# Rotating queries and keys with neighbouring pairs, a swap in two transfers, and another order of normalising

## The reference, cut to what matters

```python
h = layernorm(x) * ln_scale + ln_bias
c_q, c_kv = h @ w_down_q.T, h @ w_down_kv.T            # latents, 128 wide
q, k, v = c_q @ w_up_q.T, c_kv @ w_up_k.T, c_kv @ w_up_v.T   # 16 heads of 64
e, o = q[..., 0::2], q[..., 1::2]                      # the same for k
q = stack([e * cos - o * sin, e * sin + o * cos], -1)  # rotary, all 64 columns
out = softmax(q @ k.T / 8) @ v @ w_out.T + x
```

## Time and profile before

| | us |
|---|---|
| median of 3 runs | 1969.89 (1966.94 to 1970.7) |
| the profiled execution's own time | 1970.43 |
| its span, first to last instruction | 1968.7 |
| loop of `stage_a` in it | about 223 to 1151 |
| busy PE, DVE, ACT, POOL in 216 to 1136 | 887, 603, 391, 771 |

### The profile page before, as it was taken

One profiled execution on the slowest core, in us unless ns is written; L12 is line 12 of the kernel. 1 busy time (PEld: TensorE's weight loads), 2 busy tenths in 40 slices (PEclk: granted clock), 3 DMA queues, 4 the chain that ended last, 5 costly groups with the idle time before them and its releaser, 6 DMA issues. The chain is left out here.

```text
span 1968.7 us, 35663 instructions
## 1 busy us (share of the span) xinstructions
PE 1796.7 (91%) x12884; PEld 1290.1 (66%) x12884; DVE 1222.3 (62%) x1863; ACT 941.0 (48%) x1613; POOL 1255.2 (64%) x816
## 2 busy tenths in 40 slices
PE   5999699998999999999999978988975999998998
PEld 4888344554555555555555546666654999998998
DVE  5676566666666666756667537767752666655343
ACT  5876344434344443444434324333322567775554
POOL 3463599877788888888889734554651654435433
PEclk9999899999999999999999999999986999999999
DMA  4333322233231323332232221222336233323232
GB/s 146 107 124 125 94 50 70 59 88 97 76 86 33 97 65 76 87 76 63 56 88 67 50 92 57 81 78 82 86 99 250 44 81 93 87 44 82 40 47 40
DMA packets 92930, 160.63 MB, mean 82 GB/s; under 512 B 16188, under 2 KB 66652, under 8 KB 89428
## 3 DMA queue, kind: packets, MB, share of 16 engines
q1 hardware_dynamic: 73920, 121.69, 22.7%
q0 software_dynamic: 14592, 18.40, 5.6%
q10 hardware_dynamic: 4288, 18.81, 2.6%
HBM read 80.06 MB, written 44.71 MB: 63 GB/s over the span
## 5 line engine op out<-in xcount | busy, mean ns | idle before, releaser
L1215 ACT ACTIVATE a_pr<-a_pT 128x1024 f32<-128x1024 f32 x256 | 262.6, 1026 | 421.7 <-PE a_pT L954 421.7
L1073 DVE TENSOR_REDUCE a_row_max<-a_pG 128x2 f32<-128x1024 f32 x256 | 310.4, 1215 | 110.7 <-PE a_pG L924 110.5
L1250 POOL TENSOR_TENSOR a_total<-a_total,a_pr 128x1024 f32<-128x1024 f32 x128 | 316.2, 2470 | 16.1 <-ACT a_pr L1215 8.6
L2288 DVE TENSOR_TENSOR c_h_lo<-c_h,c_h_hi 128x256 fp32r<-128x256 f32 x288 | 151.7, 532 | 182.7 <-ACT c_h_hi L2243 178.0
L967 PE MATMUL a_pA<-a_pr,a_v 128*64 128x512 f32 x1024 | 248.1, 605 | 0.0
L2243 ACT ACTIVATE c_h<-c_pU,c_b_c 128x256 f32<-128x256 f32 x288 | 141.3, 491 | 172.0 <-PE c_pU L105 171.0
L1231 POOL TENSOR_TENSOR a_by_cos<-a_by_cos,a_swapped 128x1024 f32<-128x1024 f32 x64 | 151.6, 2369 | 105.6 <-DMA a_swapped<-a_by_sin 105.6
L1250 POOL TENSOR_TENSOR a_total<-a_pr 128x1024 f32<-128x1024 f32 x64 | 166.3, 2598 | 40.2 <-ACT a_pr L1215 40.2
L1238 POOL TENSOR_TENSOR a_qk_lo<-a_by_cos,a_qk_hi 128x1024 fp32r<-128x1024 f32 x64 | 154.7, 2418 | 2.3 <-ACT a_qk_hi L1184 2.3
L2341 POOL DMA_INDIRECT out_x<-c_y,c_ids x72 | 119.1, 1654 | 41.0 <-DVE c_y L2304 28.5
L924 PE MATMUL a_pG<-a_qk_hi 64*128 64x512 f32 x512 | 117.2, 456 | 29.9 <-ACT a_qk_hi L1184 18.5
(11 more groups left out here) (297 smaller groups left out, 4861.0 us busy)
## 6 DMA issues: line engine op xcount, KB each, us to landing
a_swapped<-a_by_sin SPq DMA_DIRECT2D x256, 128.0 KB, 2.3
a_inv_by_head<-mid_inverses SPq DMA_DIRECT2D x30, 512.0 KB, 6.5
c_raw<-in_weights ACTq DMA_DIRECT2D x5, 2048.0 KB, 8.3
c_x_t<-mid_rows SPq DMA_DIRECT2D x36, 272.0 KB, 2.8
mid_latents<-f_c_parts SPq DMA_DIRECT2D x8, 1024.0 KB, 4.7
first_latents<-mid_latents SPq DMA_DIRECT2D x8, 1024.0 KB, 5.1
f_x_t<-in_x SPq DMA_DIRECT2D x8, 512.0 KB, 3.8
mid_part<-f_out SPq DMA_DIRECT2D x16, 256.0 KB, 2.4
```

What stands on the lines that cost most here:

```text
L1073: nc.vector.reduce_max(row_max[:, u % 2, :, t], pair[:], AX.X).then_inc(read, 1)
L1215: nc.scalar.activation(pr[:, n % RP, :, :], pT[:], ACT.Exp, scale=SCALE).then_inc(exp_done, 1)
L1250: nc.gpsimd.tensor_tensor(total[:, u % RT, :, :], before, pr[:, n % RP, :, :], ALU.add).then_inc(summed, 1)
L2288: nc.vector.tensor_tensor(h_lo[:, m % RH, :], h[:, m % RH, :], h_hi[:, m % RH, :], ALU.subtract).then_inc(h_lo_done[m % RH], 1)
```

## The change: what it does

1. On the host, `w_up_q` and `w_up_k` are no longer reordered: the even and odd column of a pair lie on neighbouring partitions. The sine table has +s and -s on alternate partitions, and the cosine table is laid out to match.
2. `swap(u)` is two DMAs instead of four, each with every second partition: even ones from odd ones, and the reverse. Each moves 64 rows of 4 KB.
3. `swap(u)` waits for a new semaphore that `by_sin`'s instruction raises, not for the end of `by_cos`. The counts of `swapped_in` change from 64 to 32 per unit.
4. In DVE's order `normalise(2g)` goes from the end of k = 1 to k = 2 between `maximum(u+1, 3)` and `negate(u+1)`; `normalise(2g+1)` goes from k = 2 to k = 3, still after `maximum(u+1, 1)`. The second half of `invert` in k = 0 goes from ahead of `maximum(u+1, 3)` to behind it.

```diff
                 def swap(u):
-                    wait_read(sp, "qk", u)
+                    sp.wait_ge(sin_done, u + 1)
                     if u >= 1:
                         sp.wait_ge(rope_done, u)
-                    for i in range(4):
-                        to, frm = slice(32 * i, 32 * i + 32), slice(32 * (i ^ 1), 32 * (i ^ 1) + 32)
-                        sp.dma_start(swapped[to, :, :], by_sin[frm, :, :]).then_inc(swapped_in, 16)
+                    for i in range(2):
+                        sp.dma_start(swapped[i:P:2, :, :], by_sin[1 - i:P:2, :, :]).then_inc(swapped_in, 16)
...
-                    nc.vector.tensor_tensor(by_sin[:], pair[:], sin[:].unsqueeze(1).to_broadcast([P, 2, S]), ALU.mult)
+                    nc.vector.tensor_tensor(by_sin[:], pair[:], sin[:].unsqueeze(1).to_broadcast([P, 2, S]),
+                                            ALU.mult).then_inc(sin_done, 1)
...
                     if g >= 0 and k == 0:
                         invert(g, 0)
-                    if g >= 0 and k == 2:
+                    if g >= 0 and k == 3:
                         normalise(2 * g + 1)
                     if u + 1 < UNITS:
                         maximum(u + 1, 2)
                     what = between(u)
                     if what and what[0] == "out":
                         add_out(*what[1:])
+                    if u + 1 < UNITS:
+                        maximum(u + 1, 3)
                     if g >= 0 and k == 0:
                         invert(g, 1)
+                    if g >= 0 and k == 2:
+                        normalise(2 * g)
                     if u + 1 < UNITS:
-                        maximum(u + 1, 3)
                         negate(u + 1)
-                    if g >= 0 and k == 1:
-                        normalise(2 * g)
...
-    return (np.ascontiguousarray(np.concatenate([c, c, c, c])).astype(np.float32),
-            np.ascontiguousarray(np.concatenate([s, -s, s, -s])).astype(np.float32))
+    two = lambda e, o: np.tile(np.stack([e, o], 1).reshape(DH, S), (2, 1)).astype(np.float32)
+    return two(c, c), two(s, -s)
...
-        "wq_t": a["L0_attn_w_up_q"][rows].T,
-        "wk_t": a["L0_attn_w_up_k"][rows].T,
+        "wq_t": a["L0_attn_w_up_q"].T,
+        "wk_t": a["L0_attn_w_up_k"].T,
```

More of the change, by code:

```diff
@@ L722, in stage_a @@
         round_read = [sem(f"round_read{i}") for i in range(2)]
-        cos_done = sem("cos_done")
+        sin_done = sem("sin_done")
         swapped_in = sem("swapped_in")
@@ L1063, in rotate @@
                     if u >= 1:
-                        dve.wait_ge(swapped_in, 64 * u)
+                        dve.wait_ge(swapped_in, 32 * u)
                     if u >= 2:
                         dve.wait_ge(qk_lo_done, u - 1)
-                    nc.vector.tensor_tensor(by_sin[:], pair[:], sin[:].unsqueeze(1).to_broadcast([P, 2, S]), ALU.mult)
+                    nc.vector.tensor_tensor(by_sin[:], pair[:], sin[:].unsqueeze(1).to_broadcast([P, 2, S]),
+                                            ALU.mult).then_inc(sin_done, 1)
                     nc.vector.tensor_tensor(by_cos[:, u % 2, :, :], pair[:], cos[:].unsqueeze(1).to_broadcast([P, 2, S]),
@@ L1228, in rope @@
                 def rope(u):
-                    pool.wait_ge(swapped_in, 64 * (u + 1))
+                    pool.wait_ge(swapped_in, 32 * (u + 1))
                     wait_read(pool, "qk", u)
@@ L2418, in lay_out @@
 def lay_out(a):
-    even, odd = np.arange(0, DH, 2), np.arange(1, DH, 2)
-    rows = (DH * np.arange(H0)[:, None] + np.concatenate([even, odd])[None]).ravel()
     by_chunk = lambda m: m.reshape(-1, P, m.shape[-1]).transpose(1, 0, 2).reshape(P, -1)
```

## The result

| | before | after |
|---|---|---|
| median of 5 runs each, us | 1970.7 (1966.94 to 1973.63) | 1984.25 (1979.27 to 1988.84) |
| ratio, 95% interval | | 1.0064 (1.0041 to 1.0086) |
| profiled execution, own time / span, us | 1970.43 / 1968.7 | 1988.84 / 1987.1 |
| mean granted clock | 0.970 | 0.963 |
| first `negate` to the last (63 intervals), us | 912.8 | 929.8 |

The change makes the kernel slower, by 13.6 us in the medians and by 18.4 us between the two profiled executions. That execution of after is the slowest of its five, so part of the 18.4 is scatter. 4.1 us lie where the edit changes nothing: 0.8 ahead of the first rotation (its sines start at 206.82 instead of 206.05) and 3.3 behind the loop. 14.3 lie in the attention: the loop +17.0, the way from those sines to the first `negate` -2.65.

The account below looks back on a forecast made before the run. The prediction took PE, busy 91% of the span, as the bound, its own queue setting the time. Terms of -18.5 and +29.2 gave net +10.7, or 1981 us; the median forecast was 1980, range 1960 to 1990.

Parts of the forecast that it names:

- before the loop: PE's first scores wait 4.99 us for a chain starting with the first swap; it moves by about -2.0 us.
- `maximum` of k = 2 freed: normalise(2g), gone from the end of k = 1, no longer holds up the first maximum of k = 2: -11.0 us in all.
- k = 0 with projection: Second `invert` behind maximum(u+1, 3) gives back 0.27 us in seven such units and 0.5 in unit 4: -2.3.
- unit 18: Its `qk_hi` wait of 4.97 us has more copies queued ahead of the swap; these start later too: +0.5 us.
- (a): In p = 3, batches 1 to 7, PE's first `project_out` waits for normalise(2g+1) in k = 3: 1.5 us × 7 = +10.5.
- (b): In p = 7, maximum(u+1, 2) moves later behind `normalise`, delaying the scores of tile 3: 1.1 us × 7 = +7.6.
- first rival: POOL runs out of step, `normalise` meets no POOL instruction in k = 3: net -6 or 1964, possibly 1957 us; chance 0.2.
- `rope` is 0 to 1.9 us later than now: k = 1 swap behind later broadcasts delays `rope`, 0.5 us taken; PE pays in seven k = 2 units: +3.5.
- rival 3: TensorE's clock falls in the fourteen new stalls of 1.1 to 1.5 us, 1.4 each: about +20, 2000 us; chance 0.05.
- `negate` 1.1 late in six units: In k = 2 value units normalise(2g) waits for POOL and makes `negate` late; with half once in batch 0, +7.1 us.
- third rival of the experiments: Rival to the experiments' theory, for the whole kernel: the clock makes the loss; no size or chance given.

Follow-up runs that it names:

- e3: After, with normalise(2g+1) back in k = 2 behind maximum(u+1, 1), all else as after: 1967.36 us, ratio 0.9984 to before.
- e10: After, with each `normalise` replaced by a maximum over the same 1024 elements with a two-column result: 1944.9 us, loop 901.6; whole time not comparable.
- e4: After, with the second half of `invert` ahead of maximum(u+1, 3) again: 1970.7 us, ratio 0.9999 to before.
- e5: After, with the broadcasts of the inverses a unit later, behind the swap of k = 1: 1952.82 us, ratio 0.9908 to before.
- e6: After, with the broadcasts behind the swap of k = 1 and normalise(2g+1) back in k = 2: 1938.57 us, ratio 0.9839 to before.
- e1: After's new swap with DVE's old order: 1964.05 us, ratio 0.9959 to before.
- e2: Before's old swap (four transfers, released by the cosines) with DVE's new order: 2010.61 us, ratio 1.0204 to before.
- e12: Before's old swap, with broadcasts behind the k = 1 swap, second `invert` behind maximum(u+1, 3), both `normalise` in k = 2: 1947.19 us, ratio 0.9859 to before.
- e7b: Before's layout and four transfers, released by the sines, in DVE's new order, run again: 2005.97 us, ratio 1.0192 to before.
- e7: First execution of before's layout and four transfers, released by the sines, in DVE's new order: 3449.61 us, not comparable.

## Why the prediction held, and where not

Sizes between the two profiled executions, in us; the loss by my steps was +10.7, measured in the attention +14.3.

| step | predicted | measured | evidence |
|---|---|---|---|
| before the loop | -2.0 | -2.7 | first sines to first `negate`; first `rope` 4.3 us after its sines, 6.6 in before |
| `maximum` of k = 2 freed, p = 6, seven units | -4.7 | -4.6 | unit lengths; the waits of units 14 and 46 are gone |
| k = 0 with projection, p = 4, seven units | -1.9 | -2.4 | unit lengths |
| unit 18 | +0.5 | -1.0 | unit length |
| (a), p = 3, seven units | +10.2 | +9.8 | line 990; e3, e10 |
| (b), p = 7, six units | +6.6 | +6.2 | e3, e10 |
| p = 2, six units | +3.2 | +8.2 | e4, e5 |
| batch 0 | -1.2 | +1.5 | unit 6 |
| p = 0, 1, 5 | 0 | -0.6 | |

*What held.* The decisive reading was that `normalise` is released by POOL's instruction, not by DVE's place in the order. The rows of unit 27 show the predicted arithmetic: `add_up` first, `normalise` 1.08 us past its end (1.1 from the earlier trace rows), the projection 1.52 late (1.5). e3 undoes it, and e10 shows that it is the mutual wait and not the place. In k = 3 `normalise` takes 2.51 to 2.53 us in fourteen of fifteen groups (2.05 in the last). The first rival (POOL out of step in k = 3) didn't happen: `add_up` is released by ACT here too, 0.94 us ahead.

*"In most of these units `rope` is 0 to 1.9 us later than now; I take 0.5."* This term was mis-sized. The waits for `qk_hi` in the six units p = 2 (batches 1 to 7 without unit 18) were 0.60 on the mean and are 1.77 (1.07, 2.32, 1.84, 2.05, 1.96, 1.38), so 1.2 later and not 0.5. Behind the four of at least 1.84 the clock fell, which I had given a chance of its own (rival 3) but in the wrong stalls, those of 1.0 to 1.5, where nothing of the kind came. These four units are 1.4 us longer each than their waits explain, just what rival 3 asked per stall. So p = 2 comes to +7.0 of later scores where I had +3.0, +5.7 of lower clock where I had nothing, +1.8 of late `negate` where I had +6.6, and -6.4 of freed maxima as forecast: +8.2 and not +3.2. Unit 6 is the same, a wait of 4.26 where it had 1.81, with the clock at half behind it, and 4.7 us more. I had bounded the landing in unit 41 by letting the broadcasts' 1.05 MB go through first and the swap after them at its own rate, between 324 and 191 GB/s. The traffic of unit 25 above shows otherwise: the whole 1.57 MB takes 6.9 us at 226 GB/s, with the old form 7.6 at 208, so `rope` there starts 1.5 us later in the unit than before, near the slow end of my 0 to 1.9. Behind broadcasts the new form is seen to gain 0.7 us (7.6 to 6.9), where alone it gains 1.4 (2.75 to 1.35). Why some 1.5 us pass between the end of the traffic and `rope` is open. e4 and e5 show that the queue is the cause: with the broadcasts out of the way `rope` comes 4.8 us after the sines' start in nearly every unit.

*"`negate` 1.1 late in six units."* Over-sized: it came in two of the six, 10 and 58 (`rope` 8.0 and 8.3 us after its sines), with waits of 0.65 and 0.67 (and 0.42 behind unit 6). How late `rope` of the unit before is decides. In e4 it starts 6.3 to 7.6 us after its sines, and all six units have the wait, up to 0.7, as forecast. In the other four units of after it starts 8.7 to 9.2 us after them, so the scores are late too, and `negate` is due only when `normalise`, 1.85 to 1.90 long, has ended. In e5 `rope` is on time, at 4.8, and the wait is gone as well. In e6, with `rope` as early, it is back in seven units at 0.5, since there the other `normalise` is in the same unit and makes `rope` of that unit 3.38 long.

*The two parts in isolation.* I took the swap as worth 5.2 us in either order. It is worth 8 in the old order (e1) and 26 in the new one (e2 to after), because the new order creates the very wait that a faster swap shortens. The sum came out near enough since I summed over the combined kernel, not because the parts add.

*The sizes against the runs.* The median difference, 13.6, lies between the predicted 10.7 and the 14.3 of the profiled pair. That it comes so near is partly luck: the mechanism of (a) and (b) and their sizes held (16.8 forecast, 16.0 measured), but 4.8 us of late `negate` that didn't come stand against 5.7 us of lower clock and 4.0 of later scores that I hadn't counted. The scatter of after (1979 to 1989) is wider than that of before: it has more stalls of about 2 us, and in its five runs the granted clock goes from 0.969 in the fastest to 0.963 in the slowest. That the clock makes this scatter is read from those means, not tried. The third rival of the experiments, that the clock makes the loss, is thus true of some 6 of the 14.3 us, but as a consequence of the stalls for `qk_hi`: in e5, without them, p = 2 has no such stretch.

## What to carry to other kernels

Before moving an instruction into a hole of its engine, look at what the neighbour that it shares memory with is running there: here `normalise` takes 1.2 us or 2.5 and more, and the engine's own timeline alone doesn't say which. Then follow every signal that the moved work gives, through each queue it releases: 1.75 us of `invert` moved by one instruction cost 13.5 us two engines further on, because a megabyte of broadcasts starts later ahead of a small urgent transfer on the same queue. Take such broadcasts out of the way of the urgent transfer first (e5, e12), and judge a faster transfer only in the order in which it will run.

## What the runs showed of the hardware that I had not expected

- Two transfers with every second partition of all 128 move half a MB at 388 GB/s on the mean of 1.35 us (355 to 437 in a slice, but for the first); four that each move a block of 32 partitions at 191. The form with its smaller number of transfers is worth about 22 us in the new order (e7b to after). The Trainium skill (SBUF — State Buffer, Door 1) has the first as the better case, since it spans all partitions; the trace agrees.
- With 1 MB of broadcasts ahead of it the same swap gains less: both together take 6.9 us at 226 GB/s, with the old form 7.6 at 208 (unit 25).
- A one-input `tensor_scalar` in fp32 runs 1024 elements per partition in 0.68 us but waits for POOL like one with two inputs (1.98 in k = 3); a maximum over the same data does not wait (1.21, thirty times).
- In after, stalls of PE of 2.32, 2.05, 1.96 and 1.84 us were followed by a stretch at half clock (0.62 over 4.5 us around the first); the fourteen of 1.0 to 1.5 us were not, nor was one of 1.81 in before (unit 6, granted clock 1.00 behind it).
- One execution (e7) had all of TensorE's matmuls 1.4 to 1.9 times as long, at a granted clock that reads 1.00; six later ones of the same kernel did not.
